# A two-layer transformer kernel on one Trainium2 core: half-width value projections, exponentials kept in PSUM, a wider max pass and row maxima transposed on VectorE

## Time and profile before

| | |
|---|---|
| median of 3 runs | 3055.84 us (3055.14 to 3069.56) |
| the profiled execution's own time | 3053.33 us |
| its span | 3051.5 us |
| mean granted TensorE clock | 0.949 |

### The profile page before, as it was taken

One profiled execution on the slowest core, in us unless ns is written; L12 is line 12 of the kernel. 1 busy time (PEld: TensorE's weight loads), 2 busy tenths in 40 slices (PEclk: granted clock), 3 DMA queues, 4 the chain that ended last, 5 costly groups with the idle time before them and its releaser, 6 DMA issues. The chain is left out here.

```text
span 3051.5 us, 45255 instructions
## 1 busy us (share of the span) xinstructions
PE 2749.1 (90%) x13424; PEld 2154.6 (71%) x13424; DVE 1697.5 (56%) x4308; ACT 1319.2 (43%) x2755; POOL 704.7 (23%) x528
## 2 busy tenths in 40 slices
PE   5899889989975889989989987699999999999998
PEld 4677667767754767767766765588888888888886
DVE  4777867777762677767777876422222243333333
ACT  2666656665661465555565665311111131111111
POOL 5555655555522121221221221100000000000000
PEclk8999999999976899999999998899999999999999
DMA  5445555544453455445445442421111131111100
GB/s 136 93 108 122 118 123 120 130 103 104 105 140 105 97 116 132 86 112 129 95 110 129 96 99 54 158 67 44 43 43 66 47 105 43 43 48 51 44 28 28
DMA packets 173887, 276.03 MB, mean 90 GB/s; under 512 B 29204, under 2 KB 53524, under 8 KB 173076
## 3 DMA queue, kind: packets, MB, share of 16 engines
q1 hardware_dynamic: 170772, 260.58, 35.2%
q0 software_dynamic: 2304, 12.58, 1.2%
q10 hardware_dynamic: 640, 1.05, 0.1%
HBM read 97.04 MB, written 42.99 MB: 46 GB/s over the span
## 5 line engine op out<-in xcount | busy, mean ns | idle before, releaser
L2145 DVE TENSOR_TENSOR c_product<-c_up_ps,c_gate 128x512 f32<-128x512 f32 x128 | 88.7, 693 | 653.3 <-PE c_up_ps L2211 653.3
L2199 PE MATMUL c_gate_ps<-c_h_split,c_w_split 128*128 128x512 f32 x1536 | 380.3, 396 | 22.3 <-DVE c_w_split L2097 22.3
L2183 PE MATMUL c_down_ps<-c_w_split,c_product_split 128*128 128x512 f32 x1536 | 379.3, 396 | 0.0
L2211 PE MATMUL c_up_ps<-c_h_split,c_w_split 128*128 128x512 f32 x1536 | 378.1, 394 | 0.0
L288 DVE TENSOR_TENSOR a_prob_lo<-a_prob,a_prob_hi 128x384 fp32r<-128x384 f32 (+1 forms) x384 | 310.8, 815 | 99.3 <-ACT a_prob_hi L281 96.8
L2199 PEld LDWEIGHTS c_gate_ps<-c_h_split,c_w_split 128*128 128x128 f32 x1536 | 289.1, 188 | 94.5 <-issue 24.0
L2211 PEld LDWEIGHTS c_up_ps<-c_h_split,c_w_split 128*128 128x128 f32 x1536 | 287.9, 187 | 70.5
L2183 PEld LDWEIGHTS c_down_ps<-c_w_split,c_product_split 128*128 128x128 f32 x1536 | 288.5, 188 | 69.0
L279 ACT ACTIVATE b_prob<-b_scores_t_ps 128x384 f32<-128x384 f32 (+1 forms) x384 | 201.0, 524 | 277.3 <-PE b_scores_t_ps L269 231.8
L288 DVE TENSOR_TENSOR b_prob_lo<-b_prob,b_prob_hi 128x384 fp32r<-128x384 f32 (+1 forms) x384 | 256.3, 670 | 102.0 <-ACT b_prob_hi L281 89.0
L279 ACT ACTIVATE a_prob<-a_scores_t_ps 128x384 f32<-128x384 f32 (+1 forms) x384 | 202.3, 527 | 254.2 <-PE a_scores_t_ps L269 216.0
(11 more groups left out here) (205 smaller groups left out, 4955.6 us busy)
## 6 DMA issues: line engine op xcount, KB each, us to landing
a_q_stack<-a_q_split SPq DMA_DIRECT2D x192, 128.0 KB, 3.2
a_k_stack<-a_k_split SPq DMA_DIRECT2D x192, 128.0 KB, 3.5
b_q_stack<-b_q_split SPq DMA_DIRECT2D x192, 128.0 KB, 3.2
b_k_stack<-b_k_split SPq DMA_DIRECT2D x192, 128.0 KB, 3.5
c_h_stage<-h_t SPq DMA_DIRECT2D x16, 1024.0 KB, 6.1
c_res<-x SPq DMA_DIRECT2D x16, 1024.0 KB, 5.6
c_w_stage<-in_mlp_w POOLq DMA_DIRECT2D x16, 768.0 KB, 4.6
stage<-in_x_t SPq DMA_DIRECT2D x8, 1024.0 KB, 6.2
```

Of the source, the lines that this page charges most:

```text
L2145: dve.tensor_tensor(product[:, bank, :], up_ps[:, bank, :], gate[:, bank, :], ALU.mult).then_inc(product_done, 1)
L2183: mm = pe.matmul(down_ps[:, t, :], product_split[:, kt % 2, a, t * P:t * P + P], w_split[:, w, kt, 2 * KC * P:], start=(kt == 0 and i == 0 ...
L2199: pe.matmul(gate_ps[:, bank, :], w_split[:, w, ft, c * 2 * P:c * 2 * P + P], h_split[run.pair][:, a, c, :], start=(c == 0 and w == 0 and a ...
L2211: mm = pe.matmul(up_ps[:, bank, :], w_split[:, w, ft, c * 2 * P + P:(c + 1) * 2 * P], h_split[run.pair][:, a, c, :], start=(c == 0 and w = ...
```

## The change

- Values of layer a are projected in tiles of two row blocks by eight heads: 26 matmuls of 256 columns each. Two tiles (heads 8 to 15) are made in slots 0 to 5 of the batch's own first group, and one each in slots 0 to 3 of the third and fourth groups of the batch before (heads 0 to 7). The two `lin_ps` banks are handed out by place, and the slots of the Q and K projections move. The x split and `low` of the next batch start a little earlier.
- `exp_unit` writes the high part first and then the full exponential over the scores in PSUM; `lo_unit` reads it there. `score_t_unit` k now waits for `lo_done` of k-2 in place of `exp_done`, and `exp_unit` waits for it no more.
- The max pass takes slots 1 to 11 in layer a and 1 to 9 in layer b. After units 5 and 11, `shift_made` negates and splits the maxima of two heads and transposes them in 32x32 blocks on VectorE. TensorE's transpose and ScalarE's copy and DMA are gone. SP sends them, four DMAs of 16 partitions x 128 bytes for two heads, behind `stack_send` of the same pair. A group's first `score_t_unit` waits for heads 0 and 1, its seventh for heads 2 and 3.
- In layer b the next batch's `low` moves: TensorE from slots 8 and 9 to 10 and 11 of the last group, ScalarE from its slot 10 to slot 0 of the next group, VectorE from slot 11 to slot 1 of it. `mod` gets a buffer of its own.

```diff
+SHIFTS = P // 32 * 16
...
-        self.rowmax = sb("rowmax", [P, TT, GH])
-        self.shift = sb("shift", [P, TT, 2 * GH], F32R)
-        self.shift_row = sb("shift_row", [RANK, SEQ], F32R)
+        self.rowmax = sb("rowmax", [P, GH, TT])
+        self.shift = sb("shift", [P, 2, 2, 2, TT], F32R)
+        self.shift_t = [sb(f"shift_t{i}", [P, 32]) for i in range(2)]
...
-    if k == 0:
-        apart(dve, at.ones_set, at.shift_ready, n)
+    if k % (UNITS // 2) == 0:
+        apart(dve, at.ones_set, at.shift_ready, n * 2 - 1 + k // (UNITS // 2))
...
-def shift_split(dve, at, b, g):
+def shift_made(dve, at, b, g, pair):
 
     n = number(b, g)
-    dve.wait_ge(at.score_read, (n + 1) * UNITS)
-    at_least(dve, at.shift_turned, n)
-    dve.tensor_scalar(at.shift[:, :, 0:GH], at.rowmax[:, :, :], -1.0, None, ALU.mult).then_inc(at.shift_hi, 1)
-    dve.wait_ge(at.shift_hi, n + 1)
-    dve.scalar_tensor_tensor(out=at.shift[:, :, GH:2 * GH], in0=at.rowmax[:, :, :], scalar=-1.0,
-                             in1=at.shift[:, :, 0:GH], op0=ALU.mult,
+    m = n * 2 + pair
+    heads = slice(2 * pair, 2 * pair + 2)
+    apart(dve, at.ones_set, at.score_read, n * UNITS + (pair + 1) * (UNITS // 2))
+    at_least(dve, at.shift_turned, m)
+    dve.tensor_scalar(at.shift[:, pair, 0, :, :], at.rowmax[:, heads, :], -1.0, None, ALU.mult).then_inc(at.shift_hi, 1)
+    dve.wait_ge(at.shift_hi, m + 2)
+    dve.scalar_tensor_tensor(out=at.shift[:, pair, 1, :, :], in0=at.rowmax[:, heads, :], scalar=-1.0,
+                             in1=at.shift[:, pair, 0, :, :], op0=ALU.mult,
                              op1=ALU.subtract).then_inc(at.shift_ready, 1)
-
-
-def shift_turn(pe, at, eye, b, g):
+    apart(dve, at.ones_set, at.shift_ready, m + 1)
+    at_least(dve, at.shifted[pair], n * SHIFTS)
+    dve.transpose(at.shift_t[pair][:, :],
+                  at.shift[:, :, :, :, :].rearrange("p a b c d -> p (a b c d)").bitcast(F32)).then_inc(
+        at.shift_turned, 1)
+
+
+def shift_send(sp, at, b, g, pair):
 
...
+    sp.wait_ge(at.shift_turned, n * 2 + pair + 1)
+    target = at.q_stack[g % 2][SHIFT_ROW:STACK_ROWS, 2 * pair:2 * pair + 2, :].bitcast(F32).rearrange(
+        "r h (t c i) -> r h t c i", t=TT, c=P // 32)
+    for c in range(P // 32):
+        first = 32 * c + pair * 16
+        sp.dma_start(target[:, :, :, c, :],
+                     at.shift_t[pair][first:first + 16, :]).then_inc(at.shifted[pair], 16)
...
-    if k == 0:
-        pe.wait_ge(at.shifted, n * 16 + 16)
-    at_least(pe, at.exp_done, n * UNITS + k - 1)
+    if k % (UNITS // 2) == 0:
+        pe.wait_ge(at.shifted[k // (UNITS // 2)], (n + 1) * SHIFTS)
+    at_least(pe, at.lo_done, n * UNITS + k - 1)
...
     u, w = number(b, g) * UNITS + k, WIDTH[k % 3]
     act.wait_ge(at.score_t_ready, u + 1)
-    at_least(act, at.lo_done, u - 1)
-    act.activation(at.prob[:, k % 2, 0:w], at.scores_t_ps[:, k % 2, 0:w], ACT.Exp, scale=SCALE)
     at_least(act, at.pv_done, u + 1 - at.ring)
-    act.activation(at.prob_hi[:, k % at.ring, 0:w], at.scores_t_ps[:, k % 2, 0:w], ACT.Exp,
+    act.activation(at.prob_hi[:, k % at.ring, 0:w], at.scores_t_ps[:, k % 2, 0:w], ACT.Exp, scale=SCALE)
+    act.activation(at.scores_t_ps[:, k % 2, 0:w], at.scores_t_ps[:, k % 2, 0:w], ACT.Exp,
                    scale=SCALE).then_inc(at.exp_done, 1)
 
 
 def lo_unit(dve, at, b, g, k):
     u, w = number(b, g) * UNITS + k, WIDTH[k % 3]
     dve.wait_ge(at.exp_done, u + 1)
-    dve.tensor_tensor(at.prob_lo[:, k % at.ring, 0:w], at.prob[:, k % 2, 0:w], at.prob_hi[:, k % at.ring, 0:w],
+    dve.tensor_tensor(at.prob_lo[:, k % at.ring, 0:w], at.scores_t_ps[:, k % 2, 0:w], at.prob_hi[:, k % at.ring, 0:w],
                       ALU.subtract).then_inc(at.lo_done, 1)
...
-PROJECTIONS = (((4, 7), (9, 12)), ((7, 10), (9, 12)), ((4, 7), (8, 12)), ((4, 7), (8, 12)))
+PROJECTIONS = (((6, 9), (9, 12)), ((5, 9), (9, 12)), ((4, 8), (8, 12)), ((4, 8), (8, 12)))
+LOW_SLOTS = (2, 5)
+
+
+VALUE_TILES = (((1, 0, 0, 3), (1, 1, 3, 6)), (), ((0, 0, 0, 4),), ((0, 1, 0, 4),))
+QK_PLACE = ((0, 1), (3, 4), (6, 7), (10, 11))
+VALUE_PLACE = ((2, 5), (8, 9))
+QK_PLACE_AT_FIRST = ((0, 1), (2, 3), (4, 5), (10, 11))
+VALUE_PLACE_AT_FIRST = ((6, 7), (8, 9))
+LAST_PLACE = 11
...
+def value_items(b, g, slot):
+
+    for half, pair, start, stop in VALUE_TILES[g]:
+        if start <= slot < stop and (half or has(b, 1)):
+            yield b + 1 - half, half, pair, share(2 * (3 * KC + 1), stop - start, slot - start)
...
-        at = Attention(nc, ctx, "a", HD, 4, (1, 2, 4, TT))
+        at = Attention(nc, ctx, "a", HD, 4, None, range(1, 12))
...
                     spread(*group(b, g, -1))
                 if not (last and g >= 2):
                     stack_send(sp, at, *group(b, g, 2), 0)
+                if not (last and g == GROUPS - 1):
+                    shift_send(sp, at, *group(b, g, 1), 0)
                 if not first:
                     store(*group(b, g, -1))
                 if not (last and g >= 2):
                     stack_send(sp, at, *group(b, g, 2), 1)
+                if not (last and g == GROUPS - 1):
+                    shift_send(sp, at, *group(b, g, 1), 1)
...
-                    if slot == 9 and not (last and g == GROUPS - 1):
-                        shift_copy(act, at, *group(b, g, 1))
-                        shift_send(act, at, *group(b, g, 1))
-                    if g == 0 and 1 <= slot <= TT:
-                        value(b, slot - 1)
+                    for tile in value_tiles(b, g, slot, "stop"):
+                        value(*tile)
                     if g == 0 and slot == 9 and not last:
                         adapter(b + 1)
-                    if g == 1 and slot < 2 and not last:
-                        for c in range(2):
-                            x_chunk(b + 1, slot * 2 + c)
-                    if g == 1 and slot == 5 and not last:
+                    if g == 0 and slot >= 10 and not last:
+                        x_chunk(b + 1, slot - 10)
+                    if g == 1 and slot == 0 and not last:
+                        for c in range(2, KC):
+                            x_chunk(b + 1, c)
+                    if g == 1 and slot == LOW_SLOTS[1] and not last:
                         low(b + 1)
...
-                        for k in score_share(slot):
+                        for k in score_share(at, slot):
                             score_max(dve, at, rowmask, *group(b, g, 1), k)
-                        if slot == SCORE_SLOTS[-1]:
-                            shift_split(dve, at, *group(b, g, 1))
+                            if k % (UNITS // 2) == UNITS // 2 - 1:
+                                shift_made(dve, at, *group(b, g, 1), k // (UNITS // 2))
...
+            def project_value(b, half, pair, items):
+
+                place = value_place(b, half, pair)
+                bank = bank_of(place)
+                cols = slice(half * 2 * P, (half + 1) * 2 * P)
+                for x in items:
+                    if x == 0:
+                        at_least(pe, lin_free[bank], turn_of(b, place))
+                    t, y = divmod(x, 3 * KC + 1)
+                    rows = slice((2 * pair + t) * P, (2 * pair + t + 1) * P)
+                    to = lin_ps[:, bank, t * 2 * P:(t + 1) * 2 * P]
...
+            def value_needed(b, g, k):
+
+                if g % 2 == 0 and k in (0, 2):
+                    place = value_place(b, g // 2, k // 2)
+                    pe.wait_ge(lin_free[bank_of(place)], turn_of(b, place) + 1)
...
                     score_t_unit(pe, at, eye, colmask, b, g, slot)
-                    if slot == 9 and not (last and g == GROUPS - 1):
-                        shift_turn(pe, at, eye, *group(b, g, 1))
                     if not (last and g == GROUPS - 1):
-                        for k in score_share(slot):
+                        for k in score_share(at, slot):
                             score_unit(pe, at, *group(b, g, 1), k)
                     if slot < 2 and not first:
                         pv_unit(pe, at, *group(b, g, -1), UNITS - 2 + slot)
-                    if g == 0 and slot < TT:
-                        project_value(b, slot)
-                    if g == 1 and 3 <= slot < 5 and not last:
-                        low(b + 1, share(3 * KC, 2, slot - 3))
+                    if g == 1 and LOW_SLOTS[0] <= slot < LOW_SLOTS[1] and not last:
+                        low(b + 1, share(3 * KC, LOW_SLOTS[1] - LOW_SLOTS[0], slot - LOW_SLOTS[0]))
+                    for tile in value_items(b, g, slot):
+                        project_value(*tile)
                     for i, (start, stop) in enumerate(PROJECTIONS[g]):
                         if start <= slot < stop and exists(b, g, AHEAD):
                             project(*group(b, g, AHEAD), i, share(3 * KC + 1, stop - start, slot - start))
                     if slot >= 2:
+                        value_needed(b, g, slot - 2)
                         pv_unit(pe, at, b, g, slot - 2)
...
```

(27 more changed lines are left out.)

210 lines of the change are left out of this document (110 added, 100 removed).

## The result

The changed kernel takes 3257.54 us (3250.7 to 3266.95, four runs) where the one before took 3055.49 in the same session: a ratio of 1.066, 95% interval 1.0634 to 1.0685. It is slower by 202 us. I had forecast 3124 and a range up to 3195. The profiled execution took 3257.56 us, the span is 3255.7.

A forecast was written before the change was run, and what follows sets the result against it. It took layers a and b as bound by TensorE, 90% busy, with SP's send chain the thing to watch. Layer a +42 and layer b +26 made +68 on 3053.33, 3121; with the median's 2.5, 3124; range 2985 to 3195.

The forecast's parts named there:

- the change appends to its end what the next group's first instruction needs: SP's chain from slot 6 through inverse sums and stack DMAs: the maxima's sends are added behind it.
- group start to slot 6, taken: Layer a, TensorE's time to slot 6: 12.6, 14.5, 11 and 11 us, estimates good to 1 us.
- slot 6 to the next group: Layer a: inversion 3.5, VectorE's maxima 1.0, stack issues 6.4, sends 2.4, landing 1.4, in all 14.7 us.
- Exponentials in PSUM: `lo_unit` falls to 600 ns; 0 taken on the path, bounded by 6 us gained; the new `lo_done` wait 0.
- Values: Layer a, values by eight heads: same columns redistributed, more value work in the third and fourth groups' slots.
- Sends, the size of one: SP's queue: 0.6 us to issue one small DMA, 2.4 for a pair of heads, ends 1.3 and 4.8.
- VectorE in front of the inversion: Slot 6 (b: 5): negation, split and transpose for heads 0 and 1, 1.0 us, between 0.5 and 3.9.
- The first group, 27.3: Layer a's first group: 12.6 us to slot 6 plus 14.7 behind it, 27.3 in all.
- one window of 1.7 us a batch: Layer a, TensorE's clock: waits at group starts add one 1.2 GHz window a batch, 1.7 us lost.
- Layer b: +26: Layer b: third group +26, late sums at the batch end +24, max pass over nine slots -24; sum +26 us.
- the dear end: Sends at 1.2 us each, SP 2.4 later in 45 places: +108, 3232 us; inside the slower case, chance 0.64.
- The marks: Signs: `shift_t` waits over 60 us, a's batches 112 us, four issues over 2 us, a's clock below 0.96.

The follow-up runs named there:

- e3: The kernel before with only the exponentials over PSUM and the wait of `score_t` on `lo_done`: 3048.8 us, ratio 0.9971.
- e1: The changed kernel with the exponentials put back in their two SBUF buffers and `score_t` waiting for `exp_done`: 3257.52 us.
- e2: The changed kernel with the maxima put back as before in both layers, and layer b's `low` in its old slots: 3022.43 us, 0.9868 of before.
- e5: The changed kernel with the second four sends of a group's maxima moved on SP's queue behind the next group's gather: 3187.18 us.
- e14: The changed kernel with the reciprocal moved ahead of the max pass and the maxima within its slot: 3204.34 us.
- e9: The kernel before with eight small DMAs more a group on SP's queue, into a buffer that nothing reads: 3185.13 us.
- e7: The changed kernel with the max pass back over seven slots in both layers, the rest kept: 3177.63 us.
- e12: The changed kernel, max pass over seven slots, all four heads' maxima turned at once and sent by four 32-row DMAs from SP: 3112.31 us.
- e11: The changed kernel, max pass over seven slots, all four heads' maxima turned at once and sent by four 32-row DMAs from ScalarE: 3042.83 us.
- e8: The changed kernel with every small DMA of the maxima issued twice, sixteen a group, the copies into a buffer that nothing reads: 3525.82 us.

## Why the prediction was wrong in size

The direction and the place were right: "the change appends to its end what the next group's first instruction needs". Layer a's terms against the means of six batches, from the starts of slot 6 and of the groups on TensorE:

| us | first | second | third | fourth group |
|---|---|---|---|---|
| group start to slot 6, taken | 12.6 | 14.5 | 11 | 11 |
| measured | 15.3 | 14.9 | 10.3 | 10.2 |
| slot 6 to the next group, taken | 14.7 | 17.2 | 14.7 | 14.7 |
| measured | 16.4 | 17.5 | 17.3 | 17.9 |

The second group's 17.2 is 14.7 and the 2.5 for `low` and `send_low`. The upper pair is 1.6 us out over the batch, the lower pair 7.8. The steps, one by one.

- **Exponentials in PSUM**: `lo_unit` was taken at 600 ns. The groups of after, against the earlier trace rows:

```profile
L282 DVE TENSOR_TENSOR b_prob_lo<-b_scores_t_ps,b_prob_hi 128x384 fp32r<-128x384 f32 (+1 forms) x384 | 227.1, 592 | 127.3 <-ACT b_scores_t_ps L275 116.4
L282 DVE TENSOR_TENSOR a_prob_lo<-a_scores_t_ps,a_prob_hi 128x384 fp32r<-128x384 f32 (+1 forms) x384 | 226.0, 590 | 103.3 <-ACT a_scores_t_ps L275 81.3
```

  Right. On the path I took 0 and a bound of -6 us; e3 gave -9 (3048.8 against 3057.49 in its session; by the interval 4 to 13), e1 nothing. The new wait on `lo_done` is 0 while the loop sets the group, as taken.
- **Values**: the agreement is luck. Without the maxima's part (e2) the first two groups came to 26.8 and 31.2 us, near my 27.3 and 31.7, but mine counted that part in. In e2 the first group is 14.7 us up to slot 6 and 12.0 behind it, where I had 12.6 and 14.7: slot 6 comes 2.1 us later than I took, and the stretch behind it is 2.7 us shorter.
- **Sends, the size of one**: right. I took 0.6 us and 2.4 for a pair; the source line in the changed kernel (min/median/max ns):

```profile
L231 SPq DMA_DIRECT2D a_q_stack<-a_shift_t x256: 596/611/745, 57.3 to 992.7; - x128
```

- **The failed step: slot 6 to the next group, 3.5 + 1.0 + 6.4 + 2.4 + 1.4 = 14.7.** It measured 513.67 - 496.53 = 17.1 in the group shown. Of this, inverse to the end of the sends is 512.59 - 503.55 = 9.0 (taken 8.8) and the landing 1.1 (1.4), both right. Slot 6 to the inverse is 7.0 where I had 3.5 + 1.0. The sum has one pair of sends, the first; **the second pair was never priced in layer a, though it stands on the same queue ahead of `gather`**, whose sums the same loop needs. It returned as `pv_copy`'s 2.33 us; e5, which takes that pair out from in front of `gather`, cut the wait for the sums from 36.6 to 8.1 us in 600. I had written of it in layer b only ("the sums come 6.9 us later"), once a batch and not in every group. I followed the chain once around and stopped at the group's start; a loop must be followed until it closes.
- **VectorE in front of the inversion: 1.0, in 0.5 to 3.9.** It took 2.2 in that group (500.37 to 502.58). e14, which jumps it, gave back 2.6 us in each of the last two groups of a, and nothing in b. I had chosen near the low end because other operations of slot 6 are short, but the instruction in question was the one that varies. One source line each of the changed kernel (min/median/max ns):

```profile
L211 DVE TENSOR_SCALAR a_shift<-a_rowmax x64: 170/904/1290, 56.6 to 990.1; 128x8 fp32r<-128x8 f32 x64
L211 DVE TENSOR_SCALAR b_shift<-b_rowmax x64: 170/172/1078, 1097.4 to 2082.0; 128x8 fp32r<-128x8 f32 x64
```

- **The first group, 27.3**: it came to 31.7, of which 2.7 us stand ahead of slot 6 and 1.7 behind it. Without the maxima's part it had lost 5 us against before (26.8 for 31.8), and the loop took them back. The group that had the most slack (e9's idle DMAs cost it nothing) had none once the values were out of it.
- **The clock: one window of 1.7 us a batch.** Granted 0.88 in a, over six batches: the time at the lower level costs an estimated 0.12 x 719.6 = 86 us, against 0.04 x 640.5 = 26 before, 60 more where I had 1.7 x 6 = 10. The clock's record has 30 stretches at the 1.2 GHz level in these 24 groups, 13 in the same six batches before: more than one a group, not one a batch. How much of the 60 us lengthened the kernel no run shows, since TensorE stands waiting in the same groups.
- **Layer b: +26.** It was +101 from the first group to the last batch, +15.2 for a batch. The second group grew by 3.3, the third by 6.4 and the first by 5.9 us; I had 3.7 for the third, 4 at the end of a batch, and nothing for the second. In the third group the part that I priced was right: from `stack_send` to the next group it takes 7.8 us for 4.3 before, 3.5 more. The other 2.9 are the later split of the queries (29.0 us into the group for 26.1). I took 24 back for the max pass: TensorE's waits for `b_rowmax` did fall from 22.0 to 0.9 us in 680, but no time came of it, and e7, with seven slots, is faster by 6 us a batch.
- **The range.** 1.2 us for a send (3232) was the dear end, and I cut the range short of it. The true price was 0.61 with twice the number in the loop, the same product, so that the dear end came within 26 us of the measured time by luck. Nor is it cutting rows that costs 1.2 us: the same gather in layer b, 16 rows out of one, took half of that in the kernel before (min/median/max ns):

```profile
L1197 SPq DMA_DIRECT2D b_sums<-b_pv_raw x32: 577/592/1197, 1050.6 to 1898.6; - x32
```

- **The marks**: batches of 119.9 in a for my 112; four issues in 2.68 us; clock 0.88; the waits for `shift_t` 14.8 us in a and 41.7 in b, 56 for "over 60". The rest of the delay had moved to `a_prob_lo`, `a_sums` and `b_sums`, which I had not named.

On the rule that I weighed: the subtraction with its first operand in PSUM took 590 and 592 ns, and the shortest in layer b is 481 ns before and after, so the Trainium skill's 62 cycles more for a PSUM source (VectorE: DVE Perf Modes, on the TRN2 errata) do not show here. Another page of it bears on the result. The Trainium skill (DMA: Bandwidth & Descriptors, the section on issuing engines that are not separate queues) says that a DMA on another engine saves only the sequencer's time to start it, "which is usually small relative to the DMA itself". The trace disagrees in the weight of it: 0.61 us of issue for 2 KB, in a queue that issues from 477.54 to 495.26, 17.7 us of a 28 us group, and 70 us of time between e12 and e11, which differ in nothing but the queue that issues and the place there.

## What to carry to other kernels

Treat a DMA queue as an engine: list its issues over one period, add their durations, and look whether it ever waits for the thing it is about to send. A queue whose wait in front of its gather is near zero has no slack, and each issue added lengthens the period by nearly its full issue time (33.5 of 39 us in e8). When a chain feeds itself (sums, inverse, sends, next group, sums), follow it until it closes, and do not read the cause off the largest wait: undoing the wait on `lo_done` changed its name and not the time.

Before transposing a small tile on VectorE and sending it in pieces, count the pieces: over the whole kernel one ScalarE DMA of eight rows behind four TensorE transposes cost less (3008 us) than four DMAs of 4 KB (3024) or eight of 2 KB. In layer a alone the four were 1.4 us a batch cheaper, so count by layer.
